# Every first-layer tile of a bias network built whole, and a second attention with transposed scores

## The reference

```
sim = einsum('bhid,bhjd->bhij', q * scale, k)
out = einsum('bhij,bhjd->bhid', softmax(sim), v)
```

## Time and profile before

| | us |
|---|---|
| median of three runs | 1402.49 (1401.1 to 1406.26) |
| the profiled execution | 1401.21 |
| its span | 1399.0 |
| PE busy | 1302.2 |
| ACT busy | 967.6 |
| DVE busy | 921.5 |
| POOL busy | 748.9 |

### The profile page before, as it was taken

The page is one execution under the profiler, slowest core; times in us unless marked ns, Lnnn a source line. Parts: engine busy times, 40 slices in busy tenths (PEclk is TensorE's granted clock), DMA queues, the critical chain, the costliest instruction groups (busy, mean ns, idle before and its releaser), DMA issues.

```text
span 1399.0 us, 29958 instructions
## 1 busy us (share of the span) xinstructions
PE 1302.2 (93%) x11666; PEld 616.0 (44%) x11666; DVE 921.5 (66%) x1270; ACT 967.6 (69%) x1263; POOL 748.9 (54%) x681
## 2 busy tenths in 40 slices
PE   3169999999999999999999998799997999999998
PEld 2132222222222222222222226444454888888885
DVE  6876666666666666666666657410037999999995
ACT  3377777777777777777777773332204999999994
POOL 4166666666666666666666652200000767777772
PEclk9579999999999999999999999999999999999999
DMA  2141110111011101110111000000007222212211
GB/s 69 54 134 31 31 32 2 31 31 32 2 31 32 29 4 32 31 26 7 31 32 23 9 1 1 1 0 0 0 29 272 62 60 60 54 45 52 60 30 60
DMA packets 19922, 53.27 MB, mean 38 GB/s; under 512 B 4642, under 2 KB 7330, under 8 KB 19668
## 3 DMA queue, kind: packets, MB, share of 16 engines
q1 hardware_dynamic: 19824, 51.92, 14.1%
q10 hardware_dynamic: 4, 0.01, 0.0%
HBM read 40.95 MB, written 10.95 MB: 37 GB/s over the span
## 4 chain that ended last, share of the span: by engine, by line
PE 80%; DVE 11%; issue 3%; ACT 2%; POOL 2%; DMA 1%; SPq 1%; DVEq 0%; ACTq 0%; POOLq 0%
PE ps L898 31%; PE ps L907 17%; PE ps L889 5%; DVE aneg L773 5%; PE ps L1055 4%; PE ps L1063 4%; PE ps L1004 4%; PE ps L1014 4%; PE ps L1047 3%; DVE conv L620 2%; PE ps L1038 1%; DVE big L776 1%; POOL big L355 1%; PE ps L1026 1%; PE ps L991 1%
## 5 line engine op out<-in xcount | busy, mean ns | idle before, releaser
L898 PE MATMUL ps<-big,w 64*64 64x512 f32 x4096 | 483.5, 589 | 0.0
L479 ACT ACTIVATE big<-ps 128x1024 f32<-128x1024 f32 x256 | 262.0, 1023 | 179.0 <-PE ps L898 179.0
L674 DVE TENSOR_SCALAR big<-big 128x1024 f32<-128x1024 f32 x256 | 177.8, 694 | 263.8 <-POOL big L370 263.8
L668 DVE TENSOR_TENSOR big<-qpad,ps 128x1024 f32<-128x1024 f32 x256 | 311.0, 1215 | 7.8 <-ACT ps L458 5.4
L370 POOL TENSOR_TENSOR big<-qpad 128x1024 f32<-128x1024 f32 x128 | 244.5, 1910 | 133.2 <-PE ps L898 68.6
L370 POOL TENSOR_TENSOR big<-qpad,V 128x1024 f32<-128x1024 f32 x128 | 244.5, 1910 | 129.7 <-PE ps L898 73.5
L479 ACT ACTIVATE big<-ps,vec 128x1024 f32<-128x1024 f32 x256 | 284.0, 1109 | 0.0
L390 POOL TENSOR_TENSOR big<-BT,big 128x512 f16<-128x512 f32 x129 | 150.4, 1166 | 248.0 <-DVE big L776 248.0
L907 PE MATMUL ps<-big,w3s 128*32 128x512 f32 x2048 | 246.2, 598 | 1.3 <-ACT big L479 1.3
L898 PEld LDWEIGHTS ps<-big,w 64*64 64x64 f32 x4096 | 146.6, 133 | 205.9 <-issue 112.6
L773 DVE TENSOR_REDUCE aneg<-ps 128x1 f32<-128x1024 f32 x131 | 158.3, 1209 | 6.0 <-PE ps L1047 5.7
(11 more groups left out here) (140 smaller groups left out, 1116.5 us busy)
## 6 DMA issues: line engine op xcount, KB each, us to landing
...
h1h<-q_d SPq DMA_DIRECT2D x64, 128.0 KB, 3.0
h1l<-k_d SPq DMA_DIRECT2D x64, 128.0 KB, 3.1
...
```

The lines of the kernel that those rows point to most:

```text
L479: act.activation(h2[m % H2RING], z2[m % ZRING], ACT.Relu, bias=v("cb2") if m % 2 else 0.0).then_inc(h2_ready, 1)
L668: dve.tensor_tensor(h1[m % HRING].rearrange("p (y a b) -> p y a b", y=2, b=W), u.unsqueeze(2).to_broadcast(shape), b[:, :, HALF // W * hf: ...
L674: dve.tensor_scalar(h1[m % HRING], h1[m % HRING], 0.0, None, ALU.max).then_inc(h1_ready, 1)
L898: last = pe.matmul(z2[m % ZRING][CH * y:CH * (y + 1), HALF * x:HALF * (x + 1)], w2[CH * x:CH * (x + 1), :], h1[m % HRING][CH * x:CH * (x + ...
```

## The change

Two places are changed.

**Bias network.** All 512 first-layer tiles are built whole, as sum and relu. In every 8 tiles, tiles 1, 4 and 6 are added on DVE (`add1`, U and V1 in PSUM), the other five on POOL; the relu of every tile is DVE's. POOL waits for its own last tile in place of the relu of an earlier one. The ring has 6 tiles. `offset`, `S`, `wl1`, the bf16 parts, their DMAs and the small matmuls that prepared them are gone, and the eight weight tiles of the front are all multiplied on DVE.

**Second attention.** For each of 128 slots PE computes scores twice, from stacks of three 32-row parts: "along" (queries on partitions) only for DVE's maximum, 13 slots ahead, and "across" (keys on partitions) for the exp. The negated maxima of a head, cut into two parts by POOL, go by two DMAs into two more rows of the query stack, so that "across" comes out with the maximum subtracted. exp then gives the tile with keys on partitions, which `weigh` multiplies with V in float32 without a transpose; POOL adds two exp tiles, and `sums` multiplies this with ones once in two slots. "along" and "across" take three pairs of banks in turn. DVE divides once a head (`divide`), and SP moves the head's result into place by four DMAs (`place_head`). V gets its bias by a third matmul of one row; Q and K are projected before V. The transposes at the end are gone.

```diff
-HRING, H2RING, BURST, ZRING = 4, 8, 4, 3
...
+HRING, H2RING, BURST, ZRING = 6, 8, 4, 3
+OWN = 8
+ON_DVE = (1, 4, 6)
+Q_STACK, K_STACK = [0, 0, 1], [0, 1, 0]
+ROWS = D * len(Q_STACK)
+HEADS3, PRING, AHEAD_MAX = 3, 6, 13
+QUARTER = N // 4
+SLOTS = G * NK
...
+m_d = dram("m_d", [G, 2, N], fp32)
...
+h1x = sb("h1x", [P, 2, N])
+h1 = [big[:, 4 + i, :] for i in range(4)] + [h1x[:, i, :] for i in range(2)]
...
+PT = [big[:, 4 + i, :] for i in range(PRING)]
+PSUMS = [big[:, 11, :], BT[:, 14:16, :].rearrange("p a b -> p (a b)")]
+OT = [big[:, 10, QUARTER * i:QUARTER * (i + 1)] for i in range(2)]
+orec = [big[:, 10, QUARTER * i:QUARTER * (i + 1)] for i in (2, 3)]
...
+def along_banks(x):
+    return 2 * (x % 2 if x < AHEAD_MAX else 2 * (x - AHEAD_MAX) % 3)
+def across_banks(s):
+    return 2 * ((2 * s + 1) % 3)
+def dve_built(m):
+    return sum(1 for i in range(m) if i % OWN in ON_DVE)
+def pool_built(m):
+    return m - dve_built(m)
...
+    def load_head(n):
+        i = n % HEADS3
+        for r in range(len(Q_STACK)):
+            sp.dma_start(QS[i][D * r:D * (r + 1), :].bitcast(fp32), q_d[Q_STACK[r], D * n:D * (n + 1), :]).then_inc(st_in[i], 16)
+            sp.dma_start(KS[i][D * r:D * (r + 1), :].bitcast(fp32), k_d[K_STACK[r], D * n:D * (n + 1), :]).then_inc(st_in[i], 16)
+    def move_max(n):
+        sp.wait_ge(m_lo, n + 1)
+        sp.dma_start(m_d[n].rearrange("a (q t) -> q a t", t=NK), mparts[n % HEADS3][:, :, :].bitcast(fp32)).then_inc(m_out, 16)
+        sp.wait_ge(m_out, 16 * (n + 1))
+        sp.dma_start(QS[n % HEADS3][ROWS:ROWS + 2, :].bitcast(fp32), m_d[n]).then_inc(m_in, 16)
+    def place_head(n):
+        sp.wait_ge(o_done, n + 1)
+        row, t = D * (n % HP), n // HP
+        for c in range(4):
+            sp.dma_start(rT[row:row + D, t, QUARTER * c:QUARTER * (c + 1)], OT[n % 2][D * c:D * (c + 1), :]).then_inc(rT_in[n % 2], 16)
+    for n in range(4):
         send_parts(n)
     for i in range(2):
-        sp.wait_ge(parts_out[i], 32 * 3)
-    load_head(0, 0)
-    load_head(1, 1)
-    for n in range(6, 2 * T):
+        sp.wait_ge(parts_out[i], 32 * 2)
+    for n in range(HEADS3):
+        load_head(n)
+    for n in range(4, 2 * T):
         send_parts(n)
     for i in range(2):
         sp.wait_ge(parts_out[i], 32 * T)
-    with sp.Fori(0, G // 2 - 1) as k:
...
+    for n in range(G):
+        move_max(n)
+        if n >= 2:
+            place_head(n - 2)
+        if HEADS3 <= n + 2 < G:
+            sp.wait_ge(st_ready, NK * (n + 2 - HEADS3 + 1))
+            load_head(n + 2)
+    place_head(G - 2)
+    place_head(G - 1)
...
-    for k in range(WS_POOL):
...
     pool.wait_ge(kv_ready, 1)
-    for m in range(1, PAIRS * G, 2):
-        c, w, hf = m % PAIRS // 4, m % 4 // 2, m % 2
-        if m % PIECE == 1:
+    for m in range(PAIRS * G):
+        if m % OWN not in ON_DVE:
+            c, w, hf = m % PAIRS // 4, m % 4 // 2, m % 2
             pool.wait_ge(u_ready, 2 * (m // PIECE + 1))
-        if m >= HRING:
-            pool.wait_ge(z2_ready, m - HRING + 1)
-        if m >= 2:
-            pool.wait_ge(h1_ready, m - 1)
-        shape, i = (P, 2, HALF // W, W), m // PIECE % 2
-        r5 = "p (w y c q) -> p w y c q"
-        u, a = (x[:, :].rearrange(r5, w=2, y=2, c=4)[:, w, :, c % 4, :] for x in (U[i], V2[i]))
-        pool.tensor_tensor(h1[m % HRING].rearrange("p (y a b) -> p y a b", y=2, b=W), u.unsqueeze(2).to_broadcast(shape),
-                           a[:, :, HALF // W * hf:HALF // W * (hf + 1)].unsqueeze(3).to_broadcast(shape),
-                           ALU.add).then_inc(z1_added, 1)
+            if m >= HRING:
+                pool.wait_ge(z2_ready, m - HRING + 1)
+            if m > 0:
+                pool.wait_ge(z1_pool, pool_built(m))
+            shape, i = (P, 2, HALF // W, W), m // PIECE % 2
+            r5 = "p (w y c q) -> p w y c q"
+            u, a = (x[:, :].rearrange(r5, w=2, y=2, c=4)[:, w, :, c % 4, :] for x in (U[i], V2[i]))
+            pool.tensor_tensor(h1[m % HRING].rearrange("p (y a b) -> p y a b", y=2, b=W), u.unsqueeze(2).to_broadcast(shape),
+                               a[:, :, HALF // W * hf:HALF // W * (hf + 1)].unsqueeze(3).to_broadcast(shape),
+                               ALU.add).then_inc(z1_pool, 1)
...
+    def max_parts(n):
+        pool.wait_ge(mx_ready, NK * (n + 1))
+        if n >= HEADS3:
+            pool.wait_ge(m_out, 16 * (n - HEADS3 + 1))
+        hi, lo = (mparts[n % HEADS3][:, a, :] for a in range(2))
+        pool.tensor_copy(hi, amax[n % HEADS3][:, :]).then_inc(m_hi, 1)
+        pool.wait_ge(m_hi, n + 1)
+        pool.tensor_tensor(lo, amax[n % HEADS3][:, :], hi.bitcast(fp32), ALU.subtract).then_inc(m_lo, 1)
+    max_parts(0)
+    for j in range(SLOTS // 2):
+        if j % 4 == 1 and j // 4 + 1 < G:
+            max_parts(j // 4 + 1)
+        pool.wait_ge(pr_ready, 2 * j + 2)
+        if j >= 2:
+            pool.wait_ge(sums_done, j - 1)
+        pool.tensor_tensor(PSUMS[j % 2], PT[2 * j % PRING], PT[(2 * j + 1) % PRING], ALU.add).then_inc(added, 1)
...
+    for s in range(SLOTS):
+        act.wait_ge(st_ready, s + 1)
+        if s >= PRING:
+            act.wait_ge(pv_done, s - PRING + 1)
+            act.wait_ge(added, (s - PRING) // 2 + 1)
+        act.activation(PT[s % PRING], bank(across_banks(s), 2), ACT.Exp).then_inc(pr_ready, 1)
...
-    for k in range(WS_POOL, NK):
+    for k in range(NK):
         dve.wait_ge(hat_ready, k + 2)
         dve.tensor_tensor(wsm[:, k, :], wsm[:, k, :], hx[:, :], ALU.mult).then_inc(ws_ready, 1)
-    def bound1(m):
+    def add1(m):
         c, w, hf = m % PAIRS // 4, m % 4 // 2, m % 2
+        dve.wait_ge(u_ready, 2 * (m // PIECE) + 1)
+        dve.wait_ge(v_ready1, m // PIECE + 1)
+        if m >= HRING:
+            dve.wait_ge(z2_ready, m - HRING + 1)
         shape = (P, 2, HALF // W, W)
         r5 = "p (w y c q) -> p w y c q"
         u, b = (x.rearrange(r5, w=2, y=2, c=4)[:, w, :, c % 4, :] for x in (U[m // PIECE % 2][:, :], V1))
         dve.tensor_tensor(h1[m % HRING].rearrange("p (y a b) -> p y a b", y=2, b=W), u.unsqueeze(2).to_broadcast(shape),
-                          b[:, :, HALF // W * hf:HALF // W * (hf + 1)].unsqueeze(3).to_broadcast(shape), ALU.max).then_inc(h1_ready, 1)
+                          b[:, :, HALF // W * hf:HALF // W * (hf + 1)].unsqueeze(3).to_broadcast(shape), ALU.add).then_inc(z1_dve, 1)
     def relu1(m):
-        dve.wait_ge(z1_added, m // 2 + 1)
+        if m % OWN in ON_DVE:
+            dve.wait_ge(z1_dve, dve_built(m + 1))
+        else:
+            dve.wait_ge(z1_pool, pool_built(m + 1))
         dve.tensor_scalar(h1[m % HRING], h1[m % HRING], 0.0, None, ALU.max).then_inc(h1_ready, 1)
     dve.sem_inc(bias_saved, 1)
     dve.wait_ge(kv_ready, 1)
     for m in range(PAIRS * G + AHEAD1):
         if m < PAIRS * G:
-            if m % PIECE == 0:
-                dve.wait_ge(u_ready, 2 * m // PIECE + 1)
-                dve.wait_ge(v_ready1, m // PIECE + 1)
-            if m % 2 == 1:
-                relu1(m)
-            else:
-                if m >= HRING:
-                    dve.wait_ge(z2_ready, m - HRING + 1)
-                bound1(m)
+            if m + 1 < PAIRS * G and (m + 1) % OWN in ON_DVE:
+                add1(m + 1)
+            relu1(m)
...
+    def maxes(x):
+        n, it = x // NK, x % NK
+        dve.wait_ge(sc_ready, x + 1)
+        if it == 0 and n >= HEADS3:
+            dve.wait_ge(m_lo, n - HEADS3 + 1)
+        dve.tensor_reduce(amax[n % HEADS3][:, it:it + 1], bank(along_banks(x), 2), AX.X, ALU.max, negate=True).then_inc(mx_ready, 1)
+    def divide(n):
+        dve.wait_ge(pv_done, NK * (n + 1))
+        dve.wait_ge(sums_done, NK // 2 * (n + 1))
+        dve.reciprocal(orec[n % 2], bank(6 + n % 2)[:, QUARTER:2 * QUARTER]).then_inc(rec_done, 1)
+        dve.wait_ge(rec_done, n + 1)
+        if n >= 2:
+            dve.wait_ge(rT_in[n % 2], 64 * (n // 2))
+        dve.tensor_tensor(OT[n % 2], bank(6 + n % 2)[:, 0:QUARTER], orec[n % 2], ALU.mult).then_inc(o_done, 1)
...
+    for x in range(NK, SLOTS + 2 * NK + 1):
+        if x < SLOTS:
+            maxes(x)
+        n = (x - NK - AHEAD_MAX - 3) // NK
+        if n >= 0 and (x - NK - AHEAD_MAX - 3) % NK == 0:
+            divide(n)
...
-    def offset(m):
...
+    def value(n):
+        b, jt = n // NK, n % NK
+        if n >= 4:
+            pe.wait_ge(vv_saved, n - 3)
+        for kt in range(CT):
+            pe.matmul(bank(4 + n % 4)[:, 0:C], X[:, CT * b + kt, P * jt:P * (jt + 1)], wv[:, kt, 2, :],
+                      start=(kt == 0), stop=False)
+        last = pe.matmul(bank(4 + n % 4)[:, 0:C], one_row[0:1, :], bv[0:1, :, :].rearrange("p n d -> p (n d)"), start=False, stop=True)
+        last.then_inc(vv_ready, 1)
+    def along(x):
+        n, it = x // NK, x % NK
+        if it == 0:
+            pe.wait_ge(st_in[n % HEADS3], 96 * (n // HEADS3 + 1))
+        if AHEAD_MAX + 2 <= x:
+            pe.wait_ge(pr_ready, x - AHEAD_MAX - 1)
+        elif x >= 2:
```

(68 more changed lines are left out.)

374 lines of the change are left out of this document (54 added, 320 removed).

## The result

The changed kernel takes 1662.98 us (median of 4 runs, 1659.92 to 1665.06) against 1404.38 us for the kernel before in the same session: ratio 1.184, 95% interval 1.181 to 1.188. It is slower by 259 us. The prediction was 1747, range 1520 to 1850.

The account below looks back on a forecast made before the run. Relus and POOL adds taking turns were to bound the network, PE the attention's slots. Profiled 1401.2 - 3.6 (front) + 384 (network) - 36 (attention) = 1745.6, plus 1.3 for the median: 1747 us, range 1520 to 1850.

Parts of the forecast that it names:

- The direction and its mechanism: Bias network: DVE's relus and POOL's adds wait for each other, making the kernel slower; chance of slower 0.87.
- The rival in which they run side by side: Bias network: relu and POOL add overlap without loss, PE stays the bound, 1302 us in all; chance 0.12.
- The network's size: Bias network: 17.7 us for 8 tiles against 11.70, 6.0 us more, x 64 = 384 us more.
- the handover: Bias network: some 0.25 us added to each POOL add after a release, 1.25 us for 8 tiles.
- the pauses: Bias network: turns left empty at 3 places in 8 tiles, 0 to 2.7 us, half of it taken.
- My lower bound: Bias network: hold 0.1 us shorter for each of 13 durations, 13.8 us for 8 tiles, 134 us more.
- The rival with tight packing: Bias network: relu and POOL add exclude each other without pauses, 13.8 to 16.35 us, total 1497 to 1661; chance 0.22.
- The rival with half the clock there: Bias network: pauses drop PE to 1.2 GHz, 21.4 us for 8 tiles, 621 us more, 1983; chance 0.04.
- The front: Before the network: bf16 parts and small fold gone, DVE does all eight multiplications; network starts 3.6 us earlier.
- The attention: Second attention, first value matmul to end: 335.7 us against 371.9, 36 us less (57 less to 32 more).
- the loop at 64 us: Second attention: projections, values, first scores and the maxima's way take 64 us before the 128 slots start.
- A slot: Attention loop: PE 1.79 us plus 0.16 waiting around the division, 1.95 us, x 128 = 249.6 us.

Follow-up runs that it names:

- the filler alone: Kernel before with only the attention changed, plus 14 unused matmuls filling PE's wait before the values: 1402.04 us, ratio 0.9988.
- the values ahead: Before's network with the changed attention, SP sending projections before the other heads' loads, and four value tiles computed before PE's wait: 1391.01 us, ratio 0.990.

## Why the prediction held, and where it didn't

**The direction and its mechanism held.** The relu and POOL's add, which never met before, exclude each other, as the start of the old trace showed them do. The rival in which they run side by side would have shown relus of 694 ns; the median is 1267, the longest 2401. DVE's adds kept 1.21 us beside POOL, as foreseen.

**The network's size was off by 146 us** (+384 predicted, +238 measured; 17.7 us for 8 tiles against 15.46). The term that failed is the handover. I had added 0.25 us to each POOL add, read from the multiply of the front, which ended 2.2 us after the release. That reading compared two different operations: the 1.91 that I took off is an add with repeated inputs, while the multiply reads two full tiles. The nearest that any trace has to it undisturbed is an add of two full tiles on POOL (L391), and that takes 2.38. Against 2.38 the multiply gained 0.17 us instead of losing 0.3: read so, the old trace already showed the shorter hold. In the packed pair the turn passes before the recorded durations end: 2.32 us for what adds up to 2.60. Over 13 durations the floor is then 5 x 2.32 + 3 x 0.6 = 13.4 us where I had 15.10 + 1.25 = 16.35. That is 2.9 us too much for 8 tiles. The pauses made up for part of it: the remainder, 15.46 - 13.4 = 2.1, where I took 1.4 of the 2.7 possible. My lower bound had the shorter hold right (13.8); I took its other end. The place of the pauses was right too: POOL waits for PE in three places of 8 tiles, and halving DVE's add shortened the period. The rival with tight packing (13.8 to 16.35 us) holds the network's 15.46: it had the shorter hold right and the absence of pauses wrong. The time lies just above that rival's end (1661), but its sum counted on the attention's 36 us, which did not come, so the total says nothing for or against it.

The Trainium skill, "SBUF — State Buffer", section "A bandwidth-pool intuition that's wrong (but worth ruling out)", puts some 115 ns between a release and the next op. The sum by it was 42 us lower than mine and nearer, but still too high; the traces show no added time in the packed pairs at all, 0.28 us less than the recorded durations instead.

**PE's clock in the network** fell for short stretches only (0.98 on average from 140 to 1050, 0.93 from 800 to 850), and PE, busy for 719 of 910 us, didn't bound it. The rival with half the clock there fell.

**The front** brought 1.4 of 3.6 us. DVE's multiply (1.2) and PE's last group (1.1) took what I had for them, but the last hat before them ended 1.0 us later than in the old trace (81.84 against 80.81); in this execution PE's first work (21.97 against 20.95) starts that much later already. The other 1.1 us lie between the end of the group and the network's first matmul, 5.46 us against 4.38. I took that stretch as unchanged; from 87 to 90 us the granted clock was 0.50, and 0.97 in the old trace.

**The attention had the wrong sign**: -36 predicted, +24.3 measured, 60 us apart. The steps, from the start of the stage:
- Projections 27.6 (1263.35 to 1291), as said; the 2.4 us for the last pass were 12. I had followed SP's queue only in the loop. In front of the loop, 18 loads stand ahead of the sends on which ACT's buffers depend.
- Values and first scores: 20.9 + 4.4 predicted, and the loop at 64 us. It began at 106 (1369.46). The clock, which I took as 1 throughout from the old kernel's 0.99, is the larger part: the filler alone gave 25.7 us. With both mended, by the values ahead, the loop starts at 70 (1099.30 less 1029.69). Together this start is 42 us too short.
- A slot: 1.95 predicted, with PE at 1.79 and a wait of 0.16. In a full head it was 17.6 / 8 = 2.20, with PE at 2.05 and 0.15 of waiting. So the wait for the division was right in size, though its price was not (1.76 + 0.42 us where I had 0.84); PE's work was 0.26 too small. I priced the along tile by the old scores, whose weights lie in a row; here they have a stride, 0.71 us instead of 0.55, which is 0.16. The other 0.10 is weigh and sums (1.58 us in two slots, 1.38 predicted). The last 13 slots have no along tile and are shorter, so the loop and its draining took 271.8 us against 254.6, 17 more.
- The final projections took 18.2 instead of 17.1.

The 384 and the -36 erred in opposite directions, 146 too high and 60 too low, so the total came out 84 off. That the time lies in the range owes much to the range's width of 330 us: with the network's error alone it would have come out at 1601, with the attention's alone at 1807, both inside. A range that held the time doesn't mean that each term did.
